# Two batches, not one, summed by VectorE at the end of an attention and mixture-of-experts layer, and the kept rows of one batch more added by TensorE and ScalarE

## What is computed

```python
def _L0_ffn_ref(tgt, Wr, br, W1, b1, W2, b2, gamma, beta):
    logits = jnp.einsum('bsd,ed->bse', tgt, Wr) + br
    top_v, top_i = jax.lax.top_k(logits, 2)
    top_w = jax.nn.softmax(top_v, axis=-1)
    ...
    h = jax.nn.relu(jnp.einsum('bsd,efd->bsef', tgt, W1) + b1)
    o = jnp.einsum('bsef,edf->bsed', h, W2) + b2
    tgt2 = jnp.einsum('bsed,bse->bsd', o, router_w)
    return _layer_norm(tgt + tgt2, gamma, beta)
...
x = x + _L0_ffn_ref(_layernorm(x, axis=-1), ...)
```

## Time and profile before

| What | Value |
|---|---|
| median of three runs | 640.82 us (637.32 to 641.61) |
| the profiled execution, its own time | 639.78 us |
| its span, first to last instruction | 638.0 us |
| mean granted TensorE clock | 0.978 of full |
| TensorE matmul busy over the span | 595.6 us (93%) |
| VectorE busy | 483.0 us (76%) |
| ScalarE busy | 438.5 us (69%) |
| GpSimd busy | 230.1 us (36%) |

### The profile page before, as it was taken

One profiled execution on the slowest core, in us unless ns is written; L12 is line 12 of the kernel. 1 busy time (PEld: TensorE's weight loads), 2 busy tenths in 40 slices (PEclk: granted clock), 3 DMA queues, 4 the chain that ended last, 5 costly groups with the idle time before them and its releaser, 6 DMA issues.

```text
span 638.0 us, 12472 instructions
## 1 busy us (share of the span) xinstructions
PE 595.6 (93%) x3676; PEld 323.3 (51%) x3676; DVE 483.0 (76%) x1290; ACT 438.5 (69%) x891; POOL 230.1 (36%) x389
## 2 busy tenths in 40 slices
PE   2789899999999999999999999999989999999987
PEld 1544333343433443334434344343379999999833
DVE  3578898999899899899899989988246445555457
ACT  2635788788888878888878888778855554554325
POOL 7110010021431512512332142142177775555535
PEclk9967999999999999999999999999989999999989
DMA  7751912212312412321231231114012432222173
GB/s 196 259 163 50 201 30 75 77 43 86 109 28 83 115 41 57 94 86 30 89 98 39 89 110 27 34 54 103 20 53 68 141 93 68 77 73 68 50 263 132
DMA packets 46621, 56.97 MB, mean 89 GB/s; under 512 B 8366, under 2 KB 25818, under 8 KB 46564
## 3 DMA queue, kind: packets, MB, share of 16 engines
q1 hardware_dynamic: 40580, 45.06, 25.0%
q0 software_dynamic: 4544, 8.53, 3.9%
q10 hardware_dynamic: 1440, 2.69, 1.1%
HBM read 29.28 MB, written 27.16 MB: 88 GB/s over the span
## 4 chain that ended last, share of the span: by engine, by line
PE 61%; DVE 19%; ACT 9%; issue 4%; DMA 2%; SPq 2%; POOL 2%; DVEq 0%; ACTq 0%; POOLq 0%
PE pv_psum L1064 12%; DVE mneg L771 11%; PE st_psum L994 9%; PE s_psum L978 9%; PE y_psum L1574 6%; ACT pt L652 4%; PE y_psum L1231 3%; PE side_psum L1000 3%; PE side_psum L1026 3%; PE side_psum L1020 2%; ACT xn L670 2%; PE h_psum L1565 2%; PE h_psum L1567 2%; PE h_psum L1566 2%; DVE split L778 2%
## 5 line engine op out<-in xcount | busy, mean ns | idle before, releaser
L771 DVE TENSOR_REDUCE mneg<-s_psum 128x1 f32<-128x512 f32 x512 | 322.7, 683 | 30.3 <-PE s_psum L978 28.7
L652 ACT ACTIVATE pt<-st_psum 128x512 f32<-128x512 f32 x512 | 279.0, 598 | 68.0 <-PE st_psum L994 62.7
L978 PE MATMUL s_psum<-ks,qs 64*128 64x512 f32 x512 | 202.5, 470 | 2.9 <-DVE mneg L771 2.0
L994 PE MATMUL st_psum<-qs,ks 64*128 64x512 f32 x512 | 192.7, 454 | 9.3 <-ACT pt L652 7.7
L978 PEld LDWEIGHTS s_psum<-ks,qs 64*128 64x128 f32 x512 | 82.8, 189 | 108.3 <-DVE mneg L771 86.7
L1064 PE MATMUL pv_psum<-pt,vst 128*16 128x512 f32 x1024 | 134.2, 597 | 0.0
L994 PEld LDWEIGHTS st_psum<-qs,ks 64*128 64x128 f32 x512 | 79.3, 186 | 53.4 <-ACT pt L652 41.2
L1427 ACT ACTIVATE hid<-h_psum,b1c 128x384 f32<-128x384 f32 x68 | 36.9, 581 | 45.9 <-PE h_psum L1567 45.9
L1395 POOL DMA_INDIRECT results<-res,goal_now x51 | 49.9, 979 | 34.6 <-DVE res L1482 23.2
L511 POOL DMA_INDIRECT sent<-xrow,placeu x56 | 54.5, 974 | 16.2 <-issue 16.2
L1574 PE MATMUL y_psum<-w2t,hid 128*128 128x128 f32 x408 | 48.7, 275 | 1.1 <-DVE ysum L1476 1.1
(11 more groups left out here) (234 smaller groups left out, 814.8 us busy)
## 6 DMA issues: line engine op xcount, KB each, us to landing
parts<-split SPq DMA_DIRECT2D x48, 256.0 KB, 3.0
ks<-parts SPq DMA_DIRECT2D x128, 48.0 KB
qs<-parts SPq DMA_DIRECT2D x128, 48.0 KB
lot<-sent SPq DMA_DIRECT2D x18, 198.0 KB
sent<-tail SPq DMA_DIRECT2D x16, 198.0 KB, 5.5
xres<-in_L_attn_x_dram SPq DMA_DIRECT2D x8, 256.0 KB, 3.4
pt<-in_L_ffn_W_dram SPq DMA_DIRECT2D x1, 2048.0 KB, 14.3
got<-results SPq DMA_DIRECT2D x8, 256.0 KB, 6.4
```

The costliest lines, as they stand in the source:

```text
L652: nc.scalar.activation(pt[:, n % PT_SLOTS, (g + 2) % 4, :], st_psum[:, k % ST_BANKS, :], ACT.Exp, scale=SCALE).then_inc(exp_done, 1)
L771: nc.vector.tensor_reduce(mneg[:, (n // 4) % 2, at:at + 1], s_psum[:, k % S_BANKS, :], AX_X, ALU.max, negate=True).then_inc(max_done, 1)
L978: mm(s_psum[:, k % S_BANKS, :], qs[rows, c, P * (n % 4):P * (n % 4) + P], ks[rows, c, g, :], start=True, stop=True).then_inc(s_made, 1)
L994: mm(st_psum[:, k % ST_BANKS, :], ks[rows, c, g, P * (n % 4):P * (n % 4) + P], qs[rows, c, :], start=True, stop=True).then_inc(st_made, 1)
```

## The change

VectorE now sums batch 1 as well as batch 0 (`SUMS_ON_DVE` = 2). TensorE sums only batches 2 to 7, and as these are six and there are six banks, each has a bank of its own; all six inputs are put in ahead of the loads. `PE_ADDS` is 1, so the kept rows of batch 1 are no longer added by VectorE (L1516) but by TensorE into a bank, with a copy by ScalarE, as for batches 2 to 6. The banks for the outputs are dealt out anew, and the tile `z` is twice as large.

```diff
@@ -64,9 +64,9 @@
 ST_BANKS = 3
 PT_SLOTS = 4
 COMPLETE_LAG = 3
-PE_ADDS = 2
+PE_ADDS = 1
+SUMS_ON_DVE = 2
 Y_BANKS = 2
-SUM_BANKS = FC + Y_BANKS
 KQ_LOADS = 2 * 4 + 1
 PARTS = ((0, 0, 1), (0, 1, 0))
 LAST = GROUPS * (B - 1)
@@ -1288,7 +1288,7 @@
     moments3 = sb("moments3", [P, B, TILES, 2])
     vareps3, rstd3 = sb("vareps3", [P, B, TILES]), sb("rstd3", [P, B, TILES])
     minus_mean, shift3 = sb("minus_mean3", [P, B, TILES]), sb("shift3", [P, B, TILES])
-    z = sb("z", [P, 2, TILES, D])
+    z = sb("z", [P, SUMS_ON_DVE, 2, TILES, D])
     normed = sb("normed", [P, B, TILES, D])
 
     h_psum = psum("h_psum", FC)
@@ -1298,16 +1298,16 @@
 
     def sum_bank(b):
 
-        n = (b - 1) % SUM_BANKS
+        n = b - SUMS_ON_DVE
         return h_psum[:, n, :] if n < FC else y_psum[:, n - FC, :]
 
     def sum_of(b, j):
 
-        return sum_bank(b)[:, P * j:P * j + P] if b > 0 else z[:, 1, j, :]
+        return sum_bank(b)[:, P * j:P * j + P] if b >= SUMS_ON_DVE else z[:, b, 1, j, :]
 
     def out_bank(b):
 
-        return {2: x_psum[:, 0, :], 3: out_psum[:, 0, :], 4: sum_bank(2), 5: sum_bank(3), 6: x_psum[:, 0, :]}[b]
+        return (x_psum[:, 0, :], out_psum[:, 0, :], sum_bank(2), sum_bank(3), x_psum[:, 0, :], out_psum[:, 0, :])[b - 1]
 
     b2_loaded, y_summed = sem("b2_loaded"), sem("y_summed")
 
@@ -1486,18 +1486,18 @@
 
 
 
-        def sum_first():
-            dve.wait_ge(got_in[0], 32)
-            nc.vector.tensor_tensor(z[:, 0], got[:, 0, tiles(0), :], got[:, 1, tiles(0), :], ALU.add).then_inc(z_done, 1)
-            dve.wait_ge(z_done, 1)
-            nc.vector.tensor_tensor(z[:, 1], z[:, 0], kept.xn2[:, tiles(0), :], ALU.add).then_inc(z_done, 1)
-            dve.wait_ge(z_done, 2)
+        def sum_rows(b):
+            dve.wait_ge(got_in[b], 32)
+            nc.vector.tensor_tensor(z[:, b, 0], got[:, 0, tiles(b), :], got[:, 1, tiles(b), :], ALU.add).then_inc(z_done, 1)
+            dve.wait_ge(z_done, 2 * b + 1)
+            nc.vector.tensor_tensor(z[:, b, 1], z[:, b, 0], kept.xn2[:, tiles(b), :], ALU.add).then_inc(z_done, 1)
+            dve.wait_ge(z_done, 2 * b + 2)
 
         def combine(b):
-            if b == 0:
-                sum_first()
+            if b < SUMS_ON_DVE:
+                sum_rows(b)
             else:
-                dve.wait_ge(z1_done, b)
+                dve.wait_ge(z1_done, b - SUMS_ON_DVE + 1)
             for j in range(TILES):
                 ins = nc.vector.bn_stats(stats3[:, b, j, :], sum_of(b, j))
             ins.then_inc(s3_done, 1)
@@ -1576,8 +1576,6 @@
                     ins.then_inc(y_made, 1)
 
         def add_input(b):
-            if b > SUM_BANKS:
-                pe.wait_ge(n_done, b - SUM_BANKS + 1)
             mm(sum_bank(b), ident[:], kept.xn2[:, tiles(b), :].rearrange("p j d -> p (j d)"),
                start=True, stop=False)
 
@@ -1586,26 +1584,24 @@
 
         pe.wait_ge(relu_act, first[E] * FC)
         pe.wait_ge(y_summed, first[E] * HALVES + HALVES)
-        for b in range(1, SUM_BANKS + 1):
+        for b in range(SUMS_ON_DVE, B):
             add_input(b)
         pe.wait_ge(xh_done, first[E] + 1)
         pe.wait_ge(xl_done, first[E] + 1)
         for b in range(PE_ADDS, PE_ADDS + 2):
             add_residual(b)
-        for b in range(1, B):
-            if b > SUM_BANKS:
-                add_input(b)
+        for b in range(SUMS_ON_DVE, B):
             pe.wait_ge(got_in[b], 32)
             both = [got[:, k, tiles(b), :].rearrange("p j d -> p (j d)") for k in range(2)]
             mm(sum_bank(b), ident[:], both[0], start=False, stop=False)
             mm(sum_bank(b), ident[:], both[1], start=False, stop=True).then_inc(z1_done, 1)
-        for b in range(PE_ADDS + 2, B - 2):
-            pe.wait_ge(n_done, b - 2 + 1)
+        for b in (3, 4):
+            pe.wait_ge(n_done, b - 1 + 1)
             add_residual(b)
         for b in range(PE_ADDS, B - 1):
-            if b == B - 3:
-                pe.wait_ge(out_copied, 1)
-                add_residual(B - 2)
+            if b in (4, 5):
+                pe.wait_ge(out_copied, b - 4 + 1)
+                add_residual(b + 1)
             pe.wait_ge(g_done, b + 1)
             mm(out_bank(b), ident[:], normed[:, b].rearrange("p j d -> p (j d)"), start=False, stop=True)\
                 .then_inc(added_pe, 1)
```

## The result

The changed kernel has a median of 641.0 us over 20 runs (637.68 to 643.8); the kernel before, in 20 runs beside it, 638.05 us (636.3 to 641.61). The ratio is 1.0041, with a 95% interval from 1.0025 to 1.0057: slower by about 2.6 us, where I had forecast 0.6. Beside another set of runs of the kernel before, the same kernel measured 1.0034 (1.0011 to 1.0056). Some later sets hold executions of 646 us and more, a slower state that comes whatever the kernel, and the ratios leave these out.

What follows compares the result with a forecast made beforehand. The tail was taken as bound by loads, TensorE, VectorE, then ScalarE's chain. VectorE's 1.02 us lead stays unseen; ScalarE's wait costs 0.62 us: 639.78 + 0.62 = 640.4, forecast 640.5, range 637.3 to 643.7.

Steps and rivals of the forecast that it cites:

- The sign and the place: Slower by 0.62 us, lost in the tail where ScalarE's copy of batch 1 waits for TensorE's first add.
- VectorE's adds: VectorE's sum of batch 1 in the tail: 1.45 us, wholly covered by its waits for TensorE.
- Beside GpSimd: VectorE's adds running while GpSimd makes batch 0's scale: price at batch 3 between nothing and 0.15 us, taken as nothing.
- L1516 off VectorE: Kept rows of batch 1 leave VectorE between the statistics of batches 4 and 5: saves 0.73 us.
- The new wait: ScalarE's copy of batch 1 waits for TensorE's first add until 628.33, so batch 6's normalising starts 0.62 us later.
- I take 0.3 us earlier: TensorE's last half of batch 2's sum starts 0.3 us earlier, with 1.2 GHz lasting until about 616.7.
- Rival 2: Longer TensorE idle time keeps the clock down longer, to about 620.1: 2.3 us slower, 642.2 us; chance 0.2.
- the other: The main forecast for the whole kernel: 0.6 us slower through ScalarE's wait for TensorE's first add; chance 0.55.
- Rival 1: TensorE at full clock ends its first add by about 626.6, ScalarE loses nothing: 1.1 us faster, 638.8 us; chance 0.2.
- ScalarE's chain as the bound at the end: In the tail's last stage, normalising batch 5, a copy and normalising batch 6 bind; VectorE waits 0.97 us for the last.

Runs made afterwards that it cites:

- third profile of the changed kernel: The changed kernel unaltered, profiled again: 3.4 us at 1.2 GHz, span ending 27.62 us behind VectorE's first add; no ratio of its own.
- the filling: Overwritten extra products in TensorE's wait for loads: four in the changed kernel, ratio 0.9997 to the kernel before; two in the kernel before, 0.9983 and 0.9988.
- the second half alone: Kernel before with only batch 1's kept rows moved to TensorE and ScalarE, TensorE still summing batches 1 to 7: ratio 1.0015 to the kernel before.
- the kernel with the start held back: Kernel before with one added wait: TensorE starts batch 1's sum only when batch 2's loads are in; ratio 1.0060 to the kernel before.

## Why the prediction was wrong

The sign and the place were right, the size was not. Point by point:

- **VectorE's adds** were to cost 1.45 us that lie in waits for TensorE: 1.47 was measured, and it was covered, with waits of 1.72 and 1.38 us for TensorE behind it.
- **Beside GpSimd** the price was to be nothing or 0.15. GpSimd's power instruction of batch 0 took 1.36 us instead of 1.01 beside the adds, VectorE's second add was not held up:

```profile
610.85 1.36 POOL L1406 TENSOR_TENSOR rstd<-vareps,power 128x4 f32<-128x4 f32 x1
...
613.71 1.01 POOL L1406 TENSOR_TENSOR rstd<-vareps,power 128x4 f32<-128x4 f32 x1
```

- **L1516 off VectorE**, 0.73 us: the cycle from batch 4 to 5 is 1.87 where it was 2.59, so 0.72.
- **The new wait** on ScalarE: in the third profile of the changed kernel, with 3.4 us at half clock as the sum assumed and the earliest load of batch 2, the first copy was to start 17.66 us behind VectorE's first add (628.33 − 610.67), and 17.89 was measured; the normalising of batch 6 at 20.0, and 20.21 was measured; the whole was to be 0.6 us slower, and 0.3 was measured (27.62 against 27.33).
- **The step that failed** is the one that sized the half clock: "I take 0.3 us earlier", under the clock of the earlier trace rows, for TensorE's work from batch 2 to the first add. It took over a low stretch of 3.4 us from a trace in which TensorE had stood still for 2.21 us, into a kernel where it stands still for about 4. In three of four profiles the stretch was 6.8 us. With it the first add ended at 19.82 behind VectorE's first add instead of 17.63. Of these 2.2 us the clock is 1.7: the prediction has TensorE work at half clock for about 2.65 us (614.05 to 616.7), and it did for 6.0. The rest, about 0.5, is the load of batch 2, which came 3.71 behind VectorE's first add instead of 3.07 to 3.38. Against the kernel before, the sum for the last add is 2.35 for the later start, less 0.86 for one product fewer (22 for 23), plus 1.3 for 6.0 us of work at half clock instead of 3.4: 2.8, and 2.76 was measured (25.83 − 23.07).
- **Rival 2** had this with its price, 2.3 us, which is what the profile shows (29.65 − 27.33); I gave it 0.2 and gave 0.55 to the other. My reason against it, that the clock "came back at 616.7 while TensorE worked without a gap", took 4.6 us of work without a gap (612.03 to 616.7) for enough to bring it back, whatever went before. Here TensorE worked 6.0 us without a gap before it came back, while the fall stayed nearly where it was (2.9 us behind VectorE's first add against 2.6). The Trainium skill (TensorE: Matmul & The Clock Gate, What's actually happening) has the clock default to the low level and the phase vary from run to run; that both kernels show two forms each agrees with it. Rival 1 needs full clock with the late start, which no profile without filling showed; with the filling the tail is 26.03, 1.3 us under that of the kernel before with its usual 3.4, so its price of 1.1 fits a kernel with the filling, which the change has not.
- **What I misread** besides: I named ScalarE's chain as the bound at the end. ScalarE's chain did end last, but TensorE's queue had no gap from its first sum to its last add in the kernel before already. Both paths ended within 0.3 us of each other there: the last copy, behind TensorE's last add, at 634.36 and VectorE's last row, behind ScalarE's chain, at 634.58. Taking ScalarE's wait away brought 0.2 us; taking the half clock away brought 3.
- **The first time's base.** Three runs of before had a median of 640.82, twenty had 638.05. The ratio is not touched by that.

That the idle time ahead of TensorE's first sum brings the half clock is shown by two kinds of experiment: filling it (four kernels, no half clock before the last add in five profiles) and lengthening it in the kernel before (6.8 us) both moved it the way they should. Whether the idle time brings any is not settled by its length: 2.2 to 2.3 us brought 3.4 in four profiles and none in two. What makes 3.4 us into 6.8 was tried only by holding the start back, which lengthens the idle time and moves TensorE's restart at once. In the eleven profiles with half clock two things go with it, and the runs can't part them. The idle time was 2.2 to 3.9 us in the six with 3.4 us and 4.0 to 5.2 in the five with 6.8. And the clock fell between 0.5 us ahead of TensorE's first product and 1.2 us behind it in the six, and 0.7 to 2.0 us ahead of it in the five. The prediction's own idle time, 3.9 us, lies just at this border, and the two profiles that had it lost only 0.1 to 0.3 us of tail. Both patterns were found afterwards, and what places the fall stays open.

## What to carry to other kernels

Before you let TensorE start later, see whether its queue runs without a gap from there to the end. If it does, the delay can go to the end in full, whichever engine ends last (here 2.96 us of delay and 0.7 of clock made 3.68), and half clock behind the longer wait comes on top. So weigh what other engines win against a first product that has to wait for a later load. And where a wait can't be shortened, try a few products in it whose result is overwritten: here they kept the clock up and took back the 0.4%, as far as the times can tell.

## What the runs showed of the hardware

- With 2.2 to 2.3 us without a product TensorE's clock fell to 1.2 GHz in four of five profiles of the kernel before, 0.3 to 1.2 us after TensorE had started again, and not in the one of the second half alone. With 0.5 to 1.4 us (the filled kernels) it fell in none of five before the last add; with 3.9 to 5.2 us in all seven of the others, for 3.4 or 6.8 us.
- In the first profile of the changed kernel TensorE worked 6.0 us without a gap before the clock rose. I had expected no more than the 4.6 us (612.03 to 616.7) of the kernel before.
- The same load, batch 2's, let TensorE go on between 3.04 and 4.32 us behind VectorE's first add (the changed kernel's third profile and the kernel with the start held back), a spread of over 1 us with the same DMAs ahead of it.
